# Cross-attention with a mixture of experts: the order of scores and peaks, the loads of the fractions, and the engine of the norms

## The reference, cut to what matters

```python
q, k, v = proj(layernorm(x), Wq, bq), proj(ctx, Wk, bk), proj(ctx, Wv, bv)   # 16 heads each
logits = einsum('bhqd,bhkd->bhqk', q, k) * HEAD_DIM ** -0.5
D = clip(frac[:, None, :] - frac[:, :, None], -0.2, 0.2)
bias = alpha_pos * maximum(D, 0) + alpha_neg * minimum(D, 0)                 # alphas per head
probs = softmax(gamma * logits + delta * bias)
x = x + tanh(g_xattn) * ((probs @ v) @ Wo.T + bo)
x = x + tanh(g_ffn) * (shared_mlp(layernorm(x)) + top2_of_8_experts(layernorm(x)))
```

## Time and profile before

| | us |
|---|---|
| timed runs | 631.97, 631.60, 625.74 (median 631.60) |
| profiled execution | 625.72 |
| its span, first to last instruction | 623.9 |
| TensorE, busy in the span | 533.2 (85%) |
| VectorE | 414.9 (66%) |
| GpSimd | 305.6 (49%) |
| ScalarE | 293.9 (47%) |
| first to last subtract_peaks | 70.78 to 271.89 |

### The profile page before, as it was taken

One profiled execution on the slowest core, in us unless ns is written; L12 is line 12 of the kernel. 1 busy time (PEld: TensorE's weight loads), 2 busy tenths in 40 slices (PEclk: granted clock), 3 DMA queues, 4 the chain that ended last, 5 costly groups with the idle time before them and its releaser, 6 DMA issues.

```text
span 623.9 us, 17263 instructions
## 1 busy us (share of the span) xinstructions
PE 533.2 (85%) x6424; PEld 436.4 (70%) x6425; DVE 414.9 (66%) x972; ACT 293.9 (47%) x690; POOL 305.6 (49%) x217
## 2 busy tenths in 40 slices
PE   3697698889697876976978999999999999999991
PEld 0464476667575665756645666899999999999990
DVE  4788446776474846689798865776666766666660
ACT  3654144554353525344873656544444444444440
POOL 5969455745557475733767872332222222222221
PEclk9999567997796968786897999999999999999997
DMA  8400012122221212152243558532222222222221
GB/s 282 158 2 6 2 39 81 40 83 61 96 84 39 82 40 81 45 151 86 82 136 114 192 178 198 186 52 50 43 41 50 50 50 50 38 47 50 43 26 17
DMA packets 37553, 49.16 MB, mean 79 GB/s; under 512 B 8066, under 2 KB 30722, under 8 KB 37380
## 3 DMA queue, kind: packets, MB, share of 16 engines
q1 hardware_dynamic: 30356, 39.18, 21.1%
q0 software_dynamic: 7152, 9.34, 8.1%
HBM read 31.79 MB, written 16.72 MB: 78 GB/s over the span
## 4 chain that ended last, share of the span: by engine, by line
DMA 31%; PE 22%; POOL 18%; DVE 15%; issue 9%; SPq 1%; ACT 1%; POOLq 1%; DVEq 0%; ACTq 0%
PE bank L1140 20%; DMA out<-xres,idu 20%; DMA W<-frac 8%; POOL W L472 4%; POOL W L482 4%; POOL W L473 3%; POOL W L474 2%; DVE xres L1115 2%; POOL W L471 2%; POOL W L460 2%; DVE hbuf L928 1%; DMA xres<-x 1%; POOL rstd L438 1%; DVE idu L1112 1%; DVE W L885 1%
## 5 line engine op out<-in xcount | busy, mean ns | idle before, releaser
L1140 PE MATMUL bank<-W,xT 128*128 (+1 forms) x1704 | 141.5, 260 | 0.4 <-DVE xT L1096 0.4
L729 ACT ACTIVATE hbuf<-bank,b1t 128x128 f32<-128x128 f32 x312 | 89.0, 369 | 111.8 <-PE bank L1140 109.0
L555 POOL DMA_INDIRECT out<-xres,idu x39 | 60.7, 1557 | 156.1 <-DVE xres L1115 147.1
L1140 PE MATMUL bank<-W 128*128 128x17 bf16 (+3 forms) x1440 | 97.6, 219 | 37.2 <-POOL W L474 19.6
L1140 PEld LDWEIGHTS bank<-W,xT 128*128 128x128 bf16 (+1 forms) x1704 | 118.1, 102 | 15.1 <-issue 2.4
L1140 PE MATMUL bank<-xres,W 128*128 128x128 bf16 (+1 forms) x1920 | 122.6, 223 | 0.2 <-issue 0.2
L1140 PEld LDWEIGHTS bank<-xres,W 128*128 (+1 forms) x1920 | 111.8, 98 | 6.7 <-issue 0.4
L1140 PEld LDWEIGHTS bank<-W 128*128 128x128 bf16 x1440 | 71.9, 104 | 59.5 <-POOL W L474 22.4
L619 ACT ACTIVATE W<-bank 128x512 bf16<-128x512 f32 x64 | 37.3, 584 | 101.5 <-PE bank L1236 101.5
L797 DVE TENSOR_REDUCE mx<-bank 128x4 f32<-128x512 f32 x64 | 41.2, 686 | 61.5 <-PE bank L1140 61.5
L482 POOL TENSOR_TENSOR W<-stage,W 128x1024 bf16<-128x1024 f32 x28 | 60.6, 2169 | 19.7 <-ACT W L611 18.7
(11 more groups left out here) (151 smaller groups left out, 698.2 us busy)
## 6 DMA issues: line engine op xcount, KB each, us to landing
stage<-wts SPq DMA_DIRECT2D x36, 512.0 KB
xres<-xs_dram SPq DMA_DIRECT2D x39, 128.0 KB, 2.1
xs_dram<-hbuf SPq DMA_DIRECT2D x7, 645.0 KB, 6.5
W<-ctxT SPq DMA_DIRECT2D x4, 512.0 KB, 6.5
xres<-x SPq DMA_DIRECT2D x4, 512.0 KB, 8.1
out<-xres SPq DMA_DIRECT2D x4, 512.0 KB, 5.1
W<-wproj SPq DMA_DIRECT2D x4, 256.0 KB, 7.2
W<-frac SPq DMA_DIRECT2D x16, 64.0 KB, 4.6
```

Source lines behind the costliest of these rows:

```text
L555: nc.gpsimd.indirect_dma_start(out, bass.IndirectOffsetOnAxis(idu[:, par, t:t + 1], axis=0), ysb[par][t], None, compute_op=ALU.add).then_i ...
L729: ins = nc.scalar.activation(hbuf[:, q, c * TR:(c + 1) * TR], bank[UPS * par + q][:, c * TR:(c + 1) * TR], ACT.Gelu, bias=b1t[:, par, UC * ...
L1140: return nc.tensor.matmul(o, a, b, start=start, stop=stop, **kw)
```

## The change

The scores of unit u + 2 are issued at the end of unit u, behind the transposes of its probabilities, the first bank when its peaks have been moved away. turn_peaks(u + 1) stands between the two turn_probs, and ScalarE takes peaks_moved(u + 1) ahead of both probs_high. The fractions have four buffers, and SP issues load_frac(b + 2) where it issued load_frac(b); four are loaded at the start, the first two of them ahead of a weight and of two input loads. difference(b) is cut up: clip(b) (two passes) and split_difference(b) (one) on GpSimd, and between them top_part(b) on ScalarE. norm4 moves to ScalarE, between context_high and queries_high, with the product of mean and deviation made on GpSimd by two small operations (`nmr`). slopes() stands before keys_low(0), and in group 0 turn_inputs comes after project_values. The load of `row` is issued before that of x.

```diff
-        fr = [under(T) for _ in range(2)]
+        tails = hsplit[:].rearrange("p a b n -> p (a b n)")[:, 2 * DC * T4:2 * DC * T4 + 8 * T].bitcast(fp32)
+        fr = [tails[:, k * T:(k + 1) * T] for k in range(4)]
...
             def load_frac(b):
-                if b >= 2:
-                    sp.wait_ge(d_ready, b - 1)
-                sp.dma_start(fr[b % 2], frac[:, b * T:(b + 1) * T].to_broadcast([P, T])).then_inc(ld_fr[b % 2], 16)
+                if b >= 4:
+                    sp.wait_ge(d_clipped, b - 3)
+                sp.dma_start(fr[b % 4], frac[:, b * T:(b + 1) * T].to_broadcast([P, T])).then_inc(ld_fr[b % 4], 16)
...
             load_proj(1)
+            sp.dma_start(row[:], rows.to_broadcast([P, V_N])).then_inc(ld_row, 16)
             load_x(0)
-            sp.dma_start(row[:], rows.to_broadcast([P, V_N])).then_inc(ld_row, 16)
...
             sp.dma_start(col[:], cols).then_inc(ld_col, 16)
+            load_frac(0)
+            load_frac(1)
             load_proj(3)
             load_x(2)
             load_x(3)
-            load_frac(0)
-            load_frac(1)
+            load_frac(2)
+            load_frac(3)
...
             for b in range(2, B):
-                load_frac(b)
+                if b + 2 < B:
+                    load_frac(b + 2)
                 load_piece(b // 2, b % 2)
...
-            def norm4(g):
+            def deviation4(g):
                 pool.wait_ge(ln1_stat, 4 * (g + 1))
                 link(inverse_deviation(rstd1, mv1, 4 * g, 4 * g + 4))
-                if g:
-                    pool.wait_ge(xT_ps, DC * g)
-                for s in range(4):
-                    b = 4 * g + s
-                    ins = nc.gpsimd.tensor_scalar(xh[:, s * D:(s + 1) * D], xres[:, b * D:(b + 1) * D], mv1[:, b, 0:1],
-                                                  rstd1[:, b:b + 1], ALU.subtract, ALU.mult)
-                ins.then_inc(xh_ready, 1)
-
-            def difference(b):
-
-                pool.wait_ge(ld_fr[b % 2], 16 * (b // 2 + 1))
+                link(nc.gpsimd.tensor_tensor(nmr[:, 4 * g:4 * g + 4], mv1[:, 4 * g:4 * g + 4, 0], rstd1[:, 4 * g:4 * g + 4], ALU.mult))
+                nc.gpsimd.tensor_scalar(nmr[:, 4 * g:4 * g + 4], nmr[:, 4 * g:4 * g + 4], -1.0, None, ALU.mult).then_inc(ln1_rstd, 1)
+
+            def clip(b):
+
+                pool.wait_ge(ld_fr[b % 4], 16 * (b // 4 + 1))
                 fk = col[:, K_FK + 4 * b:K_FK + 4 * b + 4].rearrange("p (k o) -> p k o", o=1).to_broadcast([P, 4, T])
-                fq = fr[b % 2].rearrange("p (o t) -> p o t", o=1).to_broadcast([P, 4, T])
+                fq = fr[b % 4].rearrange("p (o t) -> p o t", o=1).to_broadcast([P, 4, T])
+                if b >= 1:
+                    pool.wait_ge(d_ready, b)
+                link(nc.gpsimd.tensor_tensor(dx.rearrange("p (k t) -> p k t", k=4), fk, fq, ALU.subtract))
+                nc.gpsimd.tensor_scalar(dx, dx, cst[:, C_FLOOR:C_FLOOR + 1], cst[:, C_CEIL:C_CEIL + 1], ALU.max, ALU.min).then_inc(d_clipped, 1)
+
+            def split_difference(b):
+
+                pool.wait_ge(d_top, b + 1)
                 if b >= 2:
                     pool.wait_ge(s_ps, R * (b - 1))
-                link(nc.gpsimd.tensor_tensor(dx.rearrange("p (k t) -> p k t", k=4), fk, fq, ALU.subtract))
-                link(nc.gpsimd.tensor_scalar(dx, dx, cst[:, C_FLOOR:C_FLOOR + 1], cst[:, C_CEIL:C_CEIL + 1], ALU.max, ALU.min))
-                link(nc.gpsimd.tensor_scalar(dtop, dx, cst[:, C_LOW:C_LOW + 1], None, ALU.mult))
                 nc.gpsimd.tensor_tensor(dblk[b % 2], dx, dtop, ALU.subtract).then_inc(d_ready, 1)
-                pool.wait_ge(d_ready, b + 1)
...
             for b in range(B):
+                if b + 1 < B:
+                    split_difference(b + 1)
                 if b + 2 < B:
-                    difference(b + 2)
+                    clip(b + 2)
                 if b < B - 1:
                     piece_low(b // 2, b % 2)
...
+            def norm4(g):
+                act.wait_ge(ln1_rstd, g + 1)
+                if g:
+                    act.wait_ge(xT_ps, DC * g)
+                for s in range(4):
+                    b = 4 * g + s
+                    ins = nc.scalar.activation(xh[:, s * D:(s + 1) * D], xres[:, b * D:(b + 1) * D], ACT.Identity,
+                                               scale=rstd1[:, b:b + 1], bias=nmr[:, b:b + 1])
+                ins.then_inc(xh_ready, 1)
+
+            def top_part(b):
+                act.wait_ge(d_clipped, b + 1)
+                if b:
+                    act.wait_ge(d_ready, b)
+                nc.scalar.activation(dtop, dx, ACT.Copy, scale=cst[:, C_LOW:C_LOW + 1]).then_inc(d_top, 1)
...
                 if g + 2 < Q4:
                     context_high(g + 2)
+                if g + 1 < Q4:
+                    norm4(g + 1)
+                else:
+                    top_part(0)
                 for o in range(DC):
                     queries_high(g, o)
...
                 exponent(2 * u + 1)
-                probs_high(2 * u)
                 if u + 1 < 2 * B:
                     peaks_moved(u + 1)
+                probs_high(2 * u)
                 probs_high(2 * u + 1)
                 if u % 2 == 0:
                     piece_high(b // 2, b % 2)
-                elif b >= 1:
-                    outputs_high(b - 1)
+                else:
+                    if b + 2 < B:
+                        top_part(b + 2)
+                    if b >= 1:
+                        outputs_high(b - 1)
...
+            weight_low(2, 1)
+            weight_low(0, 2)
+            slopes()
+            weight_low(3, 3)
...
                     for b in range(4 * g + 4, 4 * g + 8):
                         stats1(b)
-                else:
-                    slopes()
...
-                for i in range(2):
+                for i in (1, 0):
+                    if i == 0 and u:
+                        pe.wait_ge(mT_ready, u)
                     if u >= 2:
                         pe.wait_ge(probs, 2 * (u - 2) + i + 1)
...
                 project_keys(g)
-                turn_inputs(g)
+                if g:
+                    turn_inputs(g)
                 project_values(g)
+                if g == 0:
+                    turn_inputs(g)
                 project_queries(g)
...
             scores(0)
             turn_peaks(0)
+            scores(1)
             for u in range(2 * B):
                 b = u // 2
                 subtract_peaks(u)
-                if u + 1 < 2 * B:
-                    scores(u + 1)
...
                 turn_probs(2 * u)
-                turn_probs(2 * u + 1)
                 if u + 1 < 2 * B:
                     turn_peaks(u + 1)
+                turn_probs(2 * u + 1)
+                if u + 2 < 2 * B:
+                    scores(u + 2)
```

More of the change, by code:

```diff
@@ L185, in build @@
         rstd2 = sb("rstd2", [P, B])
+        nmr = sb("nmr", [P, B])
         mhalf = sb("mhalf", [P, B])
@@ L231, in build @@
         ld_ct = [sem(f"ld_ct{k}") for k in range(2)]
-        ld_fr = [sem(f"ld_fr{k}") for k in range(2)]
+        ld_fr = [sem(f"ld_fr{k}") for k in range(4)]
         ld_brow, brow_zero = sem("ld_brow"), sem("brow_zero")
@@ L245, in build @@
         table_ready, slope_ready, d_ready = sem("table_ready"), sem("slope_ready"), sem("d_ready")
+        d_clipped, d_top = sem("d_clipped"), sem("d_top")
         s_ps, peak, m_ready, mT_ps, mT_ready = sem("s_ps"), sem("peak"), sem("m_ready"), sem("mT_ps"), sem("mT_ready")
@@ L484, in _ @@
             context_low(0)
-            norm4(0)
+            deviation4(0)
             pool.wait_ge(ld_cst, 16)
@@ L490, in _ @@
             context_low(1)
-            norm4(1)
+            deviation4(1)
             for k in range(2):
@@ L496, in _ @@
                                   ).then_inc(table_ready, 1)
+            pool.wait_ge(ld_col, 16)
             context_low(2)
-            norm4(2)
+            deviation4(2)
+            clip(0)
             context_low(3)
-            norm4(3)
-            pool.wait_ge(ld_col, 16)
-            difference(0)
-            difference(1)
+            deviation4(3)
+            split_difference(0)
+            clip(1)
             pool.wait_ge(setup_act, 2)
@@ L637, in _ @@
             weight_high(0)
+            norm4(0)
             weight_high(3)
@@ L655, in _ @@
             act.wait_ge(ld_col, 16)
+            top_part(1)
             peaks_moved(0)
@@ L852, in slot @@
                     aggregate2(*LN2[0])
-            dve.wait_ge(ld_cst, 16)
-            nc.vector.tensor_copy(idb[:], ident)
-            nc.vector.memset(oneb[:], 1.0)
-            weight_low(1, 0)
-            for b in range(4):
-                stats1(b)
-            dve.wait_ge(ld_row, 16)
-            nc.vector.tensor_scalar(gs[:], row[:, V_GAMMA:V_GAMMA + 1], HD ** -0.5, None, ALU.mult).then_inc(setup_dve, 1)
-            dve.wait_ge(setup_dve, 1)
-            dve.wait_ge(ld_brow, 16)
```

(23 more changed lines are left out.)

## The result

| | before | after |
|---|---|---|
| timed runs, median | 628.87 us (625.74 to 631.97) | 586.26 us (581.57 to 588.52) |
| profiled execution, its span | 625.72, 623.9 | 587.57, 585.7 |

A forecast was written before the change was run, and what follows sets the result against it. Attention was taken to be bound by the loop of fraction loads, GpSimd and SP. Scores(0) at 70, 5.8 to the first subtract, 31 x 5.3 and 3 gave 243.1, 28.8 us earlier: 597, or 603 from the median; forecast 599, range 581 to 622.

The forecast's parts named there:

- the loop that was removed: Attention: fraction load, GpSimd's passes, piece_low and SP's issues repeat each sample, 13.95 us a sample.
- the rival of the TensorE-bound ring: Attention: VectorE's backlog stays under TensorE's 2.3 us, a unit costs 4.9 us, time 584; chance 0.22.
- a two-unit period under 9.8: Attention: sign that the prediction is wrong because VectorE had slack; 10.2 to 11 us for two units was expected.
- its ring: Attention: 2.6 us from turn_peaks through scores plus 2.7 us from scores to the next turn_peaks, 5.3 us a unit.
- the rest: Attention unit, from turn_peaks on: turn_peaks 0.22, four transposes 0.52 and scores 1.85, together 2.6 us.
- the backlog: Attention: VectorE's leftover low halves, then residual or outputs_low, start the next reductions 0.6 to 1.0 us late.
- GpSimd's hold-up: Attention: clip or piece_low draws out VectorE's small operations of the peaks' chain, 0.1 to 0.8 us; 0.2 taken.
- gapless rival: Attention: TensorE without gaps at 4.55 us a unit and the norms cheap as well, time 573; chance 0.05.
- the bound of 11 us a group: Projection stage: lower bound of the ring forecast at 13.1 us, if the norms take 0.36 us each.
- my bounds of 3.6 to 6.8: Projection stage: bounds in us for slopes() in its new place, all at the quick pace or as before; 5.7 taken.
- What follows moves along with it: Behind attention: everything after the last subtract_peaks, weight pieces too, comes earlier by the same 28.8 us.
- Half clock throughout: Attention: rival where gaps keep TensorE at 1.2 GHz, 7.0 us a unit, time 647; chance 0.06.

The follow-up runs named there:

- loads_only: Kernel before with only the fractions' part (four buffers, earlier loads, clip, top_part, split_difference) and the new order of first loads: 575.06 us, ratio 0.9205.
- best5: best4 with residual(b - 2) moved ahead of the two probs_low: 582.15 us, ratio 0.9230.
- backlog: Changed kernel with a second bn_stats of 0.43 us in each residual: 591.09 us, ratio 0.9380.
- quiet: Changed kernel without clip, top_part, split_difference and their loads from sample 2 on; later samples reuse the first two's differences: 585.86 us, ratio 0.9301.
- norms_back: Changed kernel with the norms back on GpSimd as before: 574.99 us, ratio 0.9187.
- slopes_g1: Changed kernel with slopes() moved behind values_low(1): 577.49 us, ratio 0.9225.
- best4: Kernel before with the fractions' part and the new order of scores; norms, turn_inputs and slopes() as before: 579.90 us, ratio 0.9161.

## Why the prediction was right

Forecast 599 in 581 to 622, measured 586.26. The direction and the loop that was removed were right. The steady part of attention came as in the rival of the TensorE-bound ring (4.9 us a unit, 584, held at 0.22), and by the prediction's own sign, a two-unit period under 9.8, its ring was wrong. In the terms of the profiled execution the sum was 597 and it took 587.57: 0.6 us less up to scores(0), 15.3 less in attention, 6.5 more behind it. These last 6.5 no part of the prediction had. Without them the execution would have been 581.1, at the very edge of the range, so that the time lies well inside it is in part luck.

*The loop that bounded the kernel.* Right. loads_only removes it alone and has ratio 0.9205, and with only the order changed GpSimd still waits 63.7 us for the fractions.

*The rest of the fractions' part.* top_part costs 0.70 to 0.77 (0.6 to 0.75 forecast), GpSimd is busy 6.4 us a sample, and no sample waits for fractions.

*Scores a unit ahead.* The mechanism was right: TensorE's wait for the moved peaks gave way to one for VectorE's small operation. The size was off, in the step "Together 1.7 + 0.8 + 0.2 = 2.7 us, and the unit is 2.6 + 2.7 = 5.3 us". Measured are 2.45 us from the scores to turn_peaks in the even unit and 2.31 in the odd one, and 2.48 for the rest: 4.86 a unit. By its terms, VectorE's chain takes 1.74 (1.7 forecast). GpSimd draws the small operation out by 0.10 and 0.32, 0.21 on average (0.2). The reductions start 0.62 and 0.25 us behind the scores, 0.43 on average, where I put 0.8 for the backlog. The rest is 2.48 (2.6). So of the 0.44 us too much in a unit, 0.37 is the backlog.

Two things were wrong in the way I added them as well. In the even unit the backlog and GpSimd's hold-up lie side by side: best5 takes the first away and the second fills its place (a wait of 0.61 us as before), backlog lengthens the first and the second vanishes. And I let TensorE wait in both units, where in the odd one TensorE's own work ends as late as VectorE's; quiet takes clip's hold-up away there and the pair gains 0.04 us. The steady part was thereby put 0.44 x 31 = 13.6 us too long. From scores(0) to the last subtract_peaks the sum had 173.1 us and the trace 157.8, 15.3 less: 13.6 of it are this, 0.9 the first units (5.76 + 6.09 us, 2.1 over a pair of 9.72, where I took 3), and the remaining 0.8 lies at the two ends of the stage, not taken apart. The gapless rival's 573 is 31 x 0.75 = 23.3 us less than 597 and leaves out the cheap norms that it names; with the bound of 11 us a group it would be about 567.

*The norms.* Right, and the step that counts against the change: the ring is longer on ScalarE than on GpSimd. 12.4 us a group against 13.1 forecast; the four norms at 2.07 (2.1), queries_high 1.05 (1.1). norms_back shows that the place of the norms causes it, as the period goes back to 11.4 with slopes() still in front. The Trainium skill's figure of about 93 ns for each pointer operand (page ScalarE: Activation LUTs, section What ACT_TABLE_LOAD costs) fits the 2.07 us.

*slopes().* Dearer than forecast: 7.7 us, outside my bounds of 3.6 to 6.8 because two 16-element operations last as long as GpSimd's work beside them: L889 lasts 2.39 us, to 17.78, where GpSimd's second memset ends at 17.75, and L896 1.99 us, to 20.76, where context_low(1) ends at 20.74 (L895, of the same size, takes 0.17). In loads_only, where GpSimd stands idle beside most of it, the whole of slopes() takes 3.8 us. inputs_low(0) ended at 27.5, not 25.4. This 2.1 us and the shorter period (3 x 0.7) offset each other in scores(0) at 69.42 (70 forecast), which is luck.

*The end.* "What follows moves along with it" held in the stages' order, but this execution had 6.5 us more behind attention. TensorE's idle without a releaser accounts for it in place and about in size: 11.5 us before its weight loads against 4.8 in the kernel before. What makes it is open. The change alone doesn't make it, as norms_back and slopes_g1, which have nearly all of it, do without on their chip.

*Half clock throughout* did not come: clock 1.00 from the third unit on, with 0.6 us of gaps a sample.

Left open: whether the pair would reach TensorE's 9.1 us with piece_low held back until the small operations are done. It wasn't tried. That VectorE and GpSimd exclude each other here, and that this draws L825 out, rests on the ends that agree in each sample of the steady part, in three kernels, and on backlog, where it vanishes when GpSimd is done. It agrees with the rule of the Trainium skill, page SBUF — State Buffer, section Who interferes with whom, which counts tensor_scalar, the operation of L825, among those that can take the shared ports. That the hold lasts for GpSimd's whole operation is shown only where this is a tensor_tensor. In each sample of loads_only the second small operation has GpSimd's clip pass beside it and takes 0.47 us, yet it ends 1.28 us before that pass does:

```profile
152.03 2.06 POOL L478 TENSOR_SCALAR W<-W,cst 128x512 f32<-128x512 f32 x1
...
152.34 0.47 DVE L827 SCALAR_TENSOR_TENSOR m<-mx,m 128x8 bf16<-128x8 f32 x1
```

## What to carry to other kernels

Where the chain in order of time repeats a transfer behind a queue's other waits, issue that transfer further ahead first, and measure it without the other edits: here it was worth 8% together with one GpSimd pass moved to ScalarE, and the reordering of TensorE under 1%. GpSimd's four passes and piece_low come to 8.0 us a sample, under the 9.78 of loads_only, so by this estimate the transfer was the larger part. Hold-ups that end at the same instruction count by the longest, not by their sum, so removing one shows nothing until the other is gone too. Moving work from a slow engine to a quick one can lengthen a ring, if on the quick engine it stands in front of work that used to run beside it.

## What the runs showed of the hardware

- An 8-element VectorE operation, 0.17 us alone, took 0.27, 0.49, 0.82 and 1.97 us, and each time ended within 0.04 us of a GpSimd subtraction with both inputs in SBUF (0.49: 157.89 + 0.49 = 158.38, clip's 157.32 + 1.04 = 158.36). Beside GpSimd's max/min pass with one tensor input one took 0.47 us and ended 1.28 us before that pass.
- In the shared MLP TensorE at times stood 0.5 to 1.2 us before nearly every weight load, with nothing to wait for, and ScalarE, which waits for its matmuls, up to 7.2 us at once (best4). ScalarE's idle times without a releaser come to 3.5 to 10.3 us in each of the eight profiles of the second and third group, and none in the four of the first, on another chip. The median of the kernel before was 625.5 us in that first group and 631.0 and 633.1 in the others. What makes these spells is open.
- Four 128x256 activations with pointer scale and pointer bias take 2.07 us, a 128x512 one with a pointer scale 0.70 to 0.77.
